# A fused transformer kernel: the second half of the first layernorm goes to ScalarE, its transposes stand between query projections, and the second key projection ahead of the first scores

## What is computed

```python
x = x + tanh(g_xattn[0]) * L0_xattn(layernorm(x), ctx, ctx, pos, mask, Wq, Wk, Wv, Wo)
x = x + tanh(g_ffn[0]) * L0_ffn(layernorm(x), W_q, scales, zeros, mask, scale2, bias)
# layernorm(x) = (x - mean) / sqrt(var + eps)
# L0_xattn: 32 query heads in 8 groups of 4, each group with one key/value head, D = 128;
#   q, k = rope(x @ Wq), rope(ctx @ Wk); softmax(mask(q k^T / sqrt(D))) v, then @ Wo
# L0_ffn: W = (W_q - zeros) * scales * scale2 * mask, a 512 x 512 matrix dequantised in the kernel
x = x + tanh(g_xattn[1]) * L1_xattn(layernorm(x), ctx, ...)   # plain attention over the context
x = x + tanh(g_ffn[1]) * L1_ffn(layernorm(x), ...)            # 32 experts, top 2
```

## Time and profile before

| | us |
|---|---|
| median of 3 runs | 922.22 (921.65 to 926.31) |
| the profiled execution | 924.77 |
| its span | 923.0 |
| PE busy | 842.6 (91%) |
| DVE busy | 660.6 (72%) |
| POOL busy | 426.9 (46%) |
| ACT busy | 393.8 (43%) |

### The profile page before, as it was taken

One profiled execution on the slowest core, in us unless ns is written; L12 is line 12 of the kernel. 1 busy time (PEld: TensorE's weight loads), 2 busy tenths in 40 slices (PEclk: granted clock), 3 DMA queues, 4 the chain that ended last, 5 costly groups with the idle time before them and its releaser, 6 DMA issues. The chain is left out here.

```text
span 923.0 us, 13113 instructions
## 1 busy us (share of the span) xinstructions
PE 842.6 (91%) x4337; PEld 705.8 (76%) x4337; DVE 660.6 (72%) x1303; ACT 393.8 (43%) x1005; POOL 426.9 (46%) x386
## 2 busy tenths in 40 slices
PE   5688899999999999999999999987989999989980
PEld 4576788888888888888888888866878687777860
DVE  3947588876778786787786778775463557999974
ACT  4334334423424433433533432443223446878970
POOL 5459626643634833643842643512020048875730
PEclk9979999999999999999999999998999968999995
DMA  8301200300110200110110120004200466999817
GB/s 333 150 1 46 98 17 1 114 1 1 48 68 1 103 11 0 45 69 1 57 57 0 45 91 1 1 1 186 105 1 12 177 234 198 366 344 340 314 36 274
DMA packets 23641, 91.13 MB, mean 99 GB/s; under 512 B 6576, under 2 KB 7088, under 8 KB 15776
## 3 DMA queue, kind: packets, MB, share of 16 engines
q1 hardware_dynamic: 17440, 81.00, 23.9%
q0 software_dynamic: 6144, 9.46, 2.9%
HBM read 86.23 MB, written 14.68 MB: 109 GB/s over the span
## 5 line engine op out<-in xcount | busy, mean ns | idle before, releaser
L359 POOL TENSOR_TENSOR qT<-straight,turned 128x512 f32<-128x512 f32 x64 | 82.5, 1289 | 154.7 <-DVE turned L557 154.2
L455 ACT ACTIVATE probs<-bank,negmax 128x128 f32<-128x128 f32 x256 | 90.5, 366 | 134.5 <-DVE negmax L568 134.5
L557 DVE TENSOR_TENSOR turned<-bank,sinT 64x512 f32<-64x512 f32 x160 | 110.2, 689 | 2.2
L133 PE MATMUL bank<-wo_hi,oT_hi 128*128 128x512 f32 x256 | 100.9, 394 | 8.7 <-DVE oT_lo L581 6.2
L133 PE MATMUL bank<-xT_hi,wq_hi 128*128 128x512 f32 x256 | 105.3, 411 | 2.1 <-DVE xT_lo L109 2.0
L135 PE MATMUL bank<-xT_hi,wq_lo 128*128 128x512 f32 x256 | 100.6, 393 | 0.0
L134 PE MATMUL bank<-xT_lo,wq_hi 128*128 128x512 f32 x256 | 100.4, 392 | 0.0
L135 PE MATMUL bank<-wo_hi,oT_lo 128*128 128x512 f32 x256 | 99.8, 390 | 0.0
L134 PE MATMUL bank<-wo_lo,oT_hi 128*128 128x512 f32 x256 | 99.8, 390 | 0.0
L462 ACT ACTIVATE pT_hi<-bank 128x512 fp32r<-128x512 f32 x64 | 38.3, 599 | 130.9 <-PE bank L722 130.9
L555 DVE TENSOR_TENSOR straight<-bank,cosT 128x512 f32<-128x512 f32 x80 | 55.3, 691 | 46.0 <-PE bank L135 45.4
(11 more groups left out here) (226 smaller groups left out, 2108.4 us busy)
## 6 DMA issues: line engine op xcount, KB each, us to landing
ring<-in_ew SPq DMA_DIRECT2D x28, 1024.0 KB, 8.4
raw_big<-in_wq SPq DMA_DIRECT2D x8, 1024.0 KB, 4.8
raw_big<-in_wo SPq DMA_DIRECT2D x8, 1024.0 KB, 4.8
early_w<-in_ew SPq DMA_DIRECT2D x8, 1024.0 KB, 8.5
ring<-picked SPq DMA_DIRECT2D x8, 512.0 KB, 7.3
raw_k<-in_wk SPq DMA_DIRECT2D x8, 256.0 KB, 5.0
ctx_raw<-in_ctxT SPq DMA_DIRECT2D x4, 512.0 KB, 6.0
raw_v<-in_wv SPq DMA_DIRECT2D x8, 256.0 KB, 5.0
```

The source lines that it names most:

```text
L133: nc.tensor.matmul(out_, hi, r_hi, start=start, stop=False)
L359: nc.gpsimd.tensor_tensor(dst, straight[:, k, :], turned[:, k, :], ALU.add).then_inc(rope_sum, 1)
L455: ex = nc.scalar.activation(probs[:, u % 2, h, :], bank_scores[u % 2][:, h * S:(h + 1) * S], ACT.Exp, bias=negmax[:, u % UNITS, h:h + 1], ...
L557: last = nc.vector.tensor_tensor(turned[dst, k, :], bank[src, :], sinT[src, tok], ALU.mult)
```

## The change

Nothing is computed that was not computed before, but for one small instruction. Five things differ:

1. The second half of the layernorm (tiles 4 to 7) is applied by ACT as `Identity(x * rstd + first_shift)`, four 128x512 instructions (`normalised`), in place of four `norm_apply` on DVE. DVE makes `first_shift = -mean * rstd` (128x4) for it, and the semaphore `pos_step`, now `opening_step`, tells ACT.
2. PE turns tiles 4 and 5 behind item 1 and tiles 6 and 7 behind item 2, and the second rotary table before the values f = 2; all of these stood behind the values. ACT's and DVE's halves of the work (`norm_upper`, `norm_rest`) move along, and on ACT the rounding of the query weights of heads 2 and 3 now stands behind normalisations.
3. The projection of item 5 of group 0 (`SECOND_KEYS`) stands at the end of PE's opening, ahead of the first scores, in place of behind them in step 0 of group 0. Its products and sum stay where they were.
4. `dequantise(0)` stands behind the sum of item 2 in place of item 3; it waits for the float weight only, and each quarter's last instruction for the float mask.
5. On DVE `closed_key` (the mask as bytes) stands before `values_rest(0, 3)`.

```diff
+        first_shift = sb("first_shift", [P, NB // 2])
...
+            SECOND_KEYS = 5
...
                         pool.wait_ge(f_deq, 4 * c + 3)
+                        pool.wait_ge(f_float, 2)
...
                         item_sum(0, item)
-                        if item == 3:
+                        if item == 2:
                             pool.wait_ge(f_small, 16 * 3)
-                            pool.wait_ge(f_float, 2)
+                            pool.wait_ge(f_float, 1)
                             dequantise(0)
...
+                    def normalised(t):
+                        act.wait_ge(opening_step, 4)
+                        nc.scalar.activation(xn[:, t, :], x[:, t, :], ACT.Identity, scale=rstd[:, t:t + 1],
+                                             bias=first_shift[:, t - 4:t - 3]).then_inc(ln_norm, 1)
...
                     norm_sqrt(act, 1, HALVES[1])
-                    for h in range(1, GR):
-                        queries_upper(0, h)
+                    queries_upper(0, 1)
+                    normalised(4)
+                    normalised(5)
+                    queries_upper(0, 2)
+                    norm_upper(act, 0, 4)
+                    norm_upper(act, 0, 5)
+                    normalised(6)
+                    normalised(7)
+                    queries_upper(0, 3)
+                    norm_upper(act, 0, 6)
+                    norm_upper(act, 0, 7)
+                    keep_rotary(1)
                     values_upper(0, 2)
-                    for t in HALVES[1]:
-                        norm_upper(act, 0, t)
-                    keep_rotary(1)
...
                     norm_stats(dve, 0, 1, HALVES[1])
+                    nc.vector.scalar_tensor_tensor(first_shift[:, :], meanvar[:, 4:8, 0], -1.0, rstd[:, 4:8], ALU.mult, ALU.mult).then_inc(opening_step, 1)
                     dve.wait_ge(rot_kept, 2)
                     item_products(0, 0)
-                    for t in HALVES[1]:
-                        norm_apply(dve, 0, t, xn)
                     item_products(0, 1)
+                    norm_rest(dve, 0, 4)
+                    norm_rest(dve, 0, 5)
                     item_products(0, 2)
+                    norm_rest(dve, 0, 6)
+                    norm_rest(dve, 0, 7)
                     values_rest(0, 2)
-                    for t in HALVES[1]:
-                        norm_rest(dve, 0, t)
                     item_products(0, 3)
-                    values_rest(0, 3)
                     dve.wait_ge(in_mask, 16)
                     nc.vector.tensor_scalar(closed_key[:, :, :], mask_raw[:, :, :], 0.0, None, ALU.is_equal)
+                    values_rest(0, 3)
                     item_products(0, 4)
...
                             for item in items:
-                                project(g, item)
+                                if not (isinstance(g, int) and g == 0 and item == SECOND_KEYS):
+                                    project(g, item)
...
                     project(0, 1)
+                    norm_turn(pe, 0, 4, xn)
+                    norm_turn(pe, 0, 5, xn)
                     project(0, 2)
+                    norm_turn(pe, 0, 6, xn)
+                    norm_turn(pe, 0, 7, xn)
+                    turn_rotary(1)
                     make_values(0, 2)
-                    for t in HALVES[1]:
-                        norm_turn(pe, 0, t, xn)
-                    turn_rotary(1)
                     project(0, 3)
                     make_values(0, 3)
                     project(0, 4)
+                    project(0, SECOND_KEYS)
                     pe.wait_ge(ln_lo, NB)
                     group(0, False)
```

More of the change, by code:

```diff
@@ L203, in program @@
             in_ctx = [sem(f"in_ctx{c}") for c in range(KC)]
-            pos_step, rot_turned, rot_kept, ctx_hi, ctx_lo = (
-                sem(n) for n in ("pos_step", "rot_turned", "rot_kept", "ctx_hi", "ctx_lo"))
+            opening_step, rot_turned, rot_kept, ctx_hi, ctx_lo = (
+                sem(n) for n in ("opening_step", "rot_turned", "rot_kept", "ctx_hi", "ctx_lo"))
             big_in, k_in, v_in = sem("big_in"), sem("k_in"), sem("v_in")
@@ L402, in _ @@
                     keys_rest(0)
-                    pool.wait_ge(pos_step, 3)
+                    pool.wait_ge(opening_step, 3)
                     for t in TILES:
@@ L628, in _ @@
                     dve.wait_ge(in_small, 32)
[L629 to L633, removed]
+                    nc.vector.tensor_scalar(pos_neg[:, :], pos_raw[:, :], 0.0, float(MAX_POS), ALU.is_lt, ALU.mult).then_inc(opening_step, 1)
+                    dve.wait_ge(opening_step, 1)
+                    nc.vector.tensor_tensor(pos_wrapped[:, :], pos_raw[:, :], pos_neg[:, :], ALU.add).then_inc(opening_step, 1)
+                    dve.wait_ge(opening_step, 2)
+                    nc.vector.tensor_scalar(pos_row[:, :], pos_wrapped[:, :], 0.0, float(MAX_POS - 1), ALU.max, ALU.min).then_inc(opening_step, 1)
                     for c in range(KC):
```

## The result

The changed kernel takes 916.69 us (median of 12 runs, 913.64 to 921.85); the kernel before, run beside it, 924.76 us (12 runs, 920.23 to 927.02). The ratio is **0.9919, 95% interval 0.9903 to 0.9934**: 7.5 us faster. Forecast were 11.1 us and 911.1 us, in a range of 909.0 to 916.5; the measured median lies 0.2 us above the range. (The 7.5 us follow from the ratio; the two medians differ by 8.1.) The profiled execution took 914.52 us (span 912.7), 10.3 us less than that of before.

What follows compares the result with a forecast made beforehand. PE bounds 113 to 600 us, and POOL's chain from item 5's sum leads into it. That sum, at 59.2 instead of 70.28, gains 11.1 us: 922.22 - 11.1 = 911.1 us, range 909.0 to 916.5.

Steps and rivals of the forecast that it cites:

- What bounds the kernel: PE from 113 to 600 us, busy 485.9 of 487; before it, POOL's chain from item 5's sum to unit 4's scores.
- The sum to the scores of unit 4: Opening through unit 4's scores: item 5's sum at 59.2 instead of 70.28, the chain behind it unchanged, 11.1 us won.
- ACT's price: Opening, ACT's four normalisations of tiles 4 to 7: 0.7 us each, bounds 0.55 and 1.28.
- DVE's 5.10 us: Opening, four normalisations between items 0 and 1 on DVE: 5.10 us, 1.28 each; 1.92 for four while POOL was idle.
- Half clock in the transposes: Rival, opening: sixteen transposes in a row on PE drop its clock, costing 3.1 us, so 914.2 us; chance 0.13.
- The start given back in group 0: Rival, before unit 4's scores: late PE or ACT's exponentials lose some 7 of 11 us, about 918.5; chance 0.10.
- Z to U4: POOL's full chain from item 5's sum to unit 4's scores, forecast to take the same 26.8 us.
- ACT as the bound: Rival, opening: ACT's four normalisations delay PE and POOL; at 5.4 us each the kernel takes 929.6; chance 0.03.
- whatever starts this stretch earlier ends the kernel earlier by as much: PE's busy stretch, 113 to 600 us, where nothing waits: an earlier start carries fully to the kernel's end.
- PE from unit 4's scores on as before: From unit 4's scores, forecast at 86.0 us, PE's work was to run unchanged.
- The prediction's own sign of being wrong: If item 5's sum comes at 59 and less than 9 us is won, the loss is in group 0.
- The level: Starting time of the whole kernel, a median of 922.22 us, from which 11.1 us was subtracted to get 911.1.

Runs made afterwards that it cites:

- 64 bytes: The changed kernel with `first_shift` made 64 bytes wide, four of its 16 columns used: 916.57 us, ratio 0.9922 to the kernel before.
- the second pair: The changed kernel and the kernel before, each run and traced again with no edit: 916.24 us, ratio 0.9913, and 924.46 us, ratio 0.9997.

## Why the prediction was right or wrong

**What bounds the kernel** was read rightly. The two traces of the changed kernel have what is left of the chain as it was drawn.

**The sum to the scores of unit 4** was forecast at 11.1 us and measured at 10.9 from the first query projection on. By parts: the turns 5.0, the keys 3.4, ACT's normalisation 1.8, the quarter 0.95; together 11.1, so they add up. (Taken to the scores of unit 4, the turns are 5.3 and the sum 11.5, 0.6 more than the whole; the turns and the quarter come from one execution each.)

**ACT's price** was 0.7 us forecast and 0.7 found (two take 1.52 us, and the instruction behind them starts 1.43 us after the first). **DVE's 5.10 us**, however, were not what that part saved; the text took the row at the place as the price of the instruction at that place, though it named POOL as its cause, and did not ask whether POOL would still be busy there. It would not, because the same change makes POOL wait for ACT. That did not harm the sum, since PE was followed to the end with all else in place; it harmed my expectation for the part alone.

**Half clock in the transposes** (0.13) did not happen. The sixteen transposes in a row at 37.90 and 38.77 ran at full length (1.04 us for eight), and 31 to 54 us has clock 1.00 in both traces. The sentence of the Trainium skill that the prediction weighed there (TensorE: Matmul & The Clock Gate, "PE-mode transpose") is not borne out by these rows; they cannot refute it either, with matmuls on both sides of the 2 us.

**The start given back in group 0** did not happen: Z to U4 is 26.8 in every kernel with four instructions a quarter, even where PE waited 3.9 us and fell to half clock behind it. **ACT as the bound** did not happen either.

**The step that failed** is the one that I took for granted, "whatever starts this stretch earlier ends the kernel earlier by as much", and with it "PE from unit 4's scores on as before". The diff begins with a new buffer of 16 bytes. I priced its instruction at 0.2 us and its place in memory at nothing, without a word. It costs 2.5 us, spread at 3 to 5 ns over the projections' matmuls: 10.9 - 2.5 = 8.4, and measured are 7.5 and 8.0 (ratios 0.9919 and 0.9913), with 8.4 inside both intervals. What in the new places makes these matmuls longer stays open.

The prediction's own sign of being wrong (the sum of item 5 at 59, and less than 9 us won) fired, at 59.91 and 7.5 us, but it pointed to a loss in group 0. Group 0 has none up to the scores of unit 5; the loss lies in the groups behind them, at 0.5 to 0.6 us for two groups (0.9 with 64 bytes).

**The level.** The forecast stood on 922.22 us, the median of three runs; twelve runs have 924.76. Of the 5.6 us between 911.1 and 916.7, 2.5 are this and 2.5 the addresses. Either one alone, left out, would have put the time inside the range, whose upper end it passed by 0.2 us. I had noted that the profiled execution lay 2.55 us above the three runs' median, and then trusted the three; it lay at the median of the twelve. A spread of 4.7 us among three runs should have moved the upper end of the range.

**The clock behind unit 4's scores** is a term of 1.5 us that the prediction did not have and that comes and goes: on these scores in one of the two traces of the kernel before, ahead of them in the other and in both of the changed one. The first profiled pair therefore showed 10.3 us and looked like a full success; that was in part luck, and only the second pair told the parts from the luck.

## What to carry to other kernels

When a kernel is bound by one engine for most of its time, read what a change does to that engine's mean instruction, not only to its waits: 3 to 5 ns over nearly a thousand matmuls outweigh a microsecond in the opening, and a new small buffer that moves the large ones is such a change. Put small scratch into an existing buffer, as here, so that the large ones stay where they are, and compare the unchanged loop of both traces first. The price of an instruction that a busy neighbour slows (here 5.10 us or 2.42 for the same four) depends on what the neighbour does at the instruction's new time, so read it again after the neighbours have moved.

## What the hardware showed that I had not expected

A new buffer of 16 or 64 bytes ahead of the weight buffers made two of the three 128x512 fp32r matmuls of each query projection step take 394 to 396 ns in place of 390 to 392, in five kernels with it against six without, while the output products stayed at 389 to 391 and the values' 128x256 products fell from 282 or 283 ns to 279 or 280. The granted clock behind the same wait of about 2 us was near 0.6 in one execution and 1.00 in another of the same kernel (waits of 2.07 and 1.62 us), worth 1.5 us. And the stretch of the experts, from G to the end, took 157.8 to 166.0 us in thirteen traces with the same instructions, a spread of 8.2 us, as wide as that of the changed kernel's twelve runs (913.64 to 921.85).
